# Wider VectorE reductions and ScalarE exponentials in the attention stage of a post-LN layer, and a shorter mask chain

## The reference

```python
q = (x @ wq.T) ... 32 heads of 128;  k, v = 8 heads of 128, each shared by 4 query heads; RoPE on q and k
scores = einsum('bhqd,bhkd->bhqk', q, k) / sqrt(128)
masked = where(causal, scores, NEG)
chunk_max = masked.reshape(b, 32, s, s // 16, 16).max(axis=-1)     # maxima over 16 keys
topk_idx = top_k(chunk_max, 8)                                     # 8 best chunks per query
allowed = causal & (in one of the 8 chunks | k_pos < 128 | k_pos > q_pos - 128)
attn = softmax(where(allowed, scores, NEG))
x = layernorm(x + (attn @ v) @ wo.T)
G = softmax gates of the 16 best of 64 adapters per token (x @ Wr.T)
x = layernorm(x + 2 * sum over adapters of (x @ A.T * G) @ B)
```

## Time and profile before

| what | us |
|---|---|
| median of 2 timed runs (6370.9 and 6371.92) | 6371.41 |
| the profiled execution, its own time | 6302.62 |
| its span, slowest core (core 0) | 6301.0 |
| span of the other cores | 6252.9 to 6294.9 |
| mean granted TensorE clock of core 0 | 0.683 |

### The profile page before, as it was taken

One profiled execution on the slowest core, in us unless ns is written; L12 is line 12 of the kernel. 1 busy time (PEld: TensorE's weight loads), 2 busy tenths in 40 slices (PEclk: granted clock), 3 DMA queues, 4 the chain that ended last, 5 costly groups with the idle time before them and its releaser, 6 DMA issues.

```text
span 6301.0 us, 53967 instructions; the slowest of 8 cores (6252.9 to 6301.0 us)
## 1 busy us (share of the span) xinstructions
PE 3229.1 (51%) x13216; PEld 1286.9 (20%) x13216; DVE 1578.1 (25%) x3829; ACT 1143.7 (18%) x2828; POOL 834.8 (13%) x1700
## 2 busy tenths in 40 slices
PE   5657665656533344445555555555677711275300
PEld 1222222222101111111111222222223311122100
DVE  1120002121343333333333333332000033211223
ACT  0000000000022233333333343443000022100011
POOL 2323332323200000000000000000122200111000
PEclk8889998889755555555555555555888955587755
DMA  7879896868500000000000000001777733464332
GB/s 125 125 108 135 131 141 103 129 104 131 84 6 2 7 1 7 1 7 1 7 1 1 7 1 7 1 1 35 160 170 165 167 122 138 122 142 76 70 133 113
DMA packets 401766, 470.92 MB, mean 75 GB/s; under 512 B 167296, under 2 KB 284032, under 8 KB 395072
## 3 DMA queue, kind: packets, MB, share of 16 engines
q0 software_dynamic: 207360, 252.27, 27.6%
q1 hardware_dynamic: 194112, 215.19, 10.9%
HBM read 652.41 MB, written 67.11 MB: 114 GB/s over the span
## 4 chain that ended last, share of the span: by engine, by line
PE 29%; DMA 23%; DVE 20%; ACT 13%; issue 12%; POOL 1%; DVEq 1%; SPq 1%; ACTq 0%; POOLq 0%; PEldq 0%
ACT Ebuf L475 6%; DMA wqt<-wqT 5%; PE pw L543 5%; PE pq L238 4%; PE pso L340 4%; PE pk L160 3%; PE psS L454 3%; DMA wkvt<-wkT 3%; DMA wkvt<-wvT 3%; DVE Cm L416 3%; ACT Ebuf L484 3%; DMA wot<-woT 3%; PE pB L818 2%; PE psS L464 2%; DVE Cm L419 2%
## 5 line engine op out<-in xcount | busy, mean ns | idle before, releaser
L160 PE MATMUL pk<-xbt,wkvt 128*128 128x512 bf16 x2048 | 504.8, 395 | 198.9 <-DMA wkvt<-wkT 86.2
L238 PE MATMUL pq<-xot,wqt 128*128 128x512 bf16 x2048 | 504.0, 394 | 180.7 <-DMA wqt<-wqT 149.0
L543 PE MATMUL pw<-oft,wot 128*128 128x512 bf16 x2048 | 471.9, 388 | 184.2 <-DMA oft<-oscr 151.6
L320 PE MATMUL ptr<-dgrz,Ebuf 128*128 128x128 bf16 x2304 | 310.2, 303 | 397.8 <-POOL dgrz L403 310.0
L377 PE MATMUL psS<-Kfm,Qfm 128*128 128x512 bf16 (+1 forms) x640 | 327.3, 534 | 285.1 <-ACT Ebuf L475 181.8
L328 ACT CAST PT<-ptr 128x512 bf16<-128x512 f32 (+1 forms) x640 | 322.6, 545 | 619.5 <-PE ptr L320 615.6
L403 POOL TENSOR_SCALAR_AFFINE_SELECT dgrz<-rzb 128x128 bf16<-128x128 bf16 x248 | 72.4, 292 | 2536.8 <-DVE rzb L400 2529.9
L475 ACT ACTIVATE Ebuf<-psS,ngm 128x512 bf16<-128x512 f32 (+2 forms) x512 | 300.5, 587 | 433.2 <-PE psS L464 398.7
L395 DVE TENSOR_REDUCE zz<-zparts 128x1 f32<-128x4 f32 (+4 forms) x248 | 38.7, 156 | 1269.0 <-ACT Ebuf L484 1269.0
L484 ACT ACTIVATE Ebuf<-psS,ngm 128x128 bf16<-128x128 f32 (+2 forms) x352 | 170.0, 483 | 957.9 <-PE psS L377 924.5
L320 PEld LDWEIGHTS ptr<-dgrz,Ebuf 128*128 128x128 bf16 x2304 | 210.1, 131 | 518.4 <-issue 509.2
(11 more groups left out here) (122 smaller groups left out, 3254.4 us busy)
## 6 DMA issues: line engine op xcount, KB each, us to landing
xot<-xoT POOLq DMA_DIRECT2D x256, 256.0 KB, 5.4
oft<-oscr SPq DMA_DIRECT2D x256, 256.0 KB, 4.6
xbt<-xbT POOLq DMA_DIRECT2D x256, 128.0 KB, 5.5
wkvt<-wkT POOLq DMA_DIRECT2D x128, 256.0 KB, 7.3
wkvt<-wvT POOLq DMA_DIRECT2D x128, 256.0 KB, 6.8
wqt<-wqT POOLq DMA_DIRECT2D x256, 128.0 KB, 6.5
wot<-woT POOLq DMA_DIRECT2D x256, 128.0 KB, 4.5
x1t<-x1Tscr SPq DMA_DIRECT2D x96, 256.0 KB, 4.0
```

What stands on the lines that cost most here:

```text
L160: ins = te.matmul(pk[kb][:], wkvt[b][:, kb * 128:(kb + 1) * 128], xbt[b][:], start=(ch == 0), stop=(ch == 31))
L238: ins = te.matmul(pq[ob * 2 + hf][:], wqt[b][:, ob * 128:(ob + 1) * 128], xot[b][:, hf * 512:(hf + 1) * 512], start=(ch == 0), stop=(ch == ...
L320: ins = te.matmul(ptr[j][:, t * 128:(t + 1) * 128], Ebuf[:, kt * 128:(kt + 1) * 128], dgrz[hp][:], start=True, stop=True)
L543: ins = te.matmul(pw[blk * 2 + hf][:], wot[b][:, blk * 128:(blk + 1) * 128], oft[b][:, hf * 512:(hf + 1) * 512], start=(ch == 0), stop=(ch ...
```

## The change

Four edits in the attention loop. The two reductions into `Cm` become one over all Nk columns. The 0/1 mask, its memset and the conversion become one compare-and-multiply that writes `mnegb` directly, followed by a memset of its first 8 chunks to 0. The exponentials of the mid part become one instruction over nmid columns, across banks. Those of the last part become one over W columns. Each bank's `bank_free` is now the last exponential that reads the bank.

```diff
-                    if nmid > 0:
-                        p.w(vec, "ST", ts)
-                        p.w(vec, "SV")
-                        src = psS[:, base: base + nmid].rearrange("p (c k) -> p c k", k=16)
-                        p.inc(vec.tensor_reduce(Cm[:, 0:ncmid], src, AX.X, ALU.max), "SV")
                     p.w(vec, "ST", ts)
                     p.w(vec, "SV")
-                    p.inc(vec.tensor_reduce(Cm[:, ncmid:nch],
-                                            psS[:, base + nmid: base + Nk].rearrange("p (c k) -> p c k", k=16),
+                    p.inc(vec.tensor_reduce(Cm[:, 0:nch],
+                                            psS[:, base: base + Nk].rearrange("p (c k) -> p c k", k=16),
                                             AX.X, ALU.max), "SV")
...
-                    p.w(vec, "SV")
-                    p.inc(vec.tensor_scalar(M01[:, 0:nch], Cm[:, 0:nch], thr[:, 0:1], None, ALU.is_ge), "SV")
-                    p.w(vec, "SV")
-                    p.inc(vec.memset(M01[:, 0:8], 1.0), "SV")
                     p.w(vec, "ST", tmt_prev)
                     p.w(vec, "SV")
-                    p.inc(vec.tensor_scalar(mnegb[:, 0:nch], M01[:, 0:nch], 1.0, 1e30,
-                                            ALU.subtract, ALU.mult), "SV")
+                    p.inc(vec.tensor_scalar(mnegb[:, 0:nch], Cm[:, 0:nch], thr[:, 0:1], -1e30,
+                                            ALU.is_lt, ALU.mult), "SV")
+                    p.w(vec, "SV")
+                    p.inc(vec.memset(mnegb[:, 0:8], 0.0), "SV")
...
-                    for (bank, off, n) in mid_banks:
+                    if nmid > 0:
                         p.w(sc, "SS")
-                        ssv = p.inc(sc.activation(Ebuf[:, off:off + n], psS[:, base + off: base + off + n],
+                        ssv = p.inc(sc.activation(Ebuf[:, 0:nmid], psS[:, base: base + nmid],
                                                   AF.Exp, bias=ngm[:, 0:1],
                                                   accum_out=zparts[:, zcol:zcol + 1]), "SS")
                         zcol += 1
-                        bank_free[(base + off) // 512] = ("SS", ssv)
-                    off = nmid
-                    while off < Nk:
-                        n = min(512 - (base + off) % 512, Nk - off)
-                        p.w(sc, "SS")
-                        ssv = p.inc(sc.activation(Ebuf[:, off:off + n], psS[:, base + off: base + off + n],
-                                                  AF.Exp, bias=ngm[:, 0:1],
-                                                  accum_out=zparts[:, zcol:zcol + 1]), "SS")
-                        zcol += 1
-                        bank_free[(base + off) // 512] = ("SS", ssv)
-                        off += n
+                        for bank in range(base // 512, (base + nmid + 511) // 512):
+                            bank_free[bank] = ("SS", ssv)
+                    p.w(sc, "SS")
+                    ssv = p.inc(sc.activation(Ebuf[:, nmid:Nk], psS[:, base + nmid: base + Nk],
+                                              AF.Exp, bias=ngm[:, 0:1],
+                                              accum_out=zparts[:, zcol:zcol + 1]), "SS")
+                    zcol += 1
+                    for bank in range((base + nmid) // 512, (base + Nk + 511) // 512):
+                        bank_free[bank] = ("SS", ssv)
```

## The result

| | before | after |
|---|---|---|
| median of the timed runs, us | 6322.07 (10 runs, 6299.84 to 6371.92) | 6064.88 (11 runs, 6049.82 to 6136.97) |
| profiled execution, us | 6302.62 | 6064.88 |
| span of the slowest core, us | 6301.0 | 6063.3 |
| mean granted clock, slowest core | 0.683 | 0.689 |
| instructions, VectorE / ScalarE | 3829 / 2828 | 3349 / 2060 |

The ratio is 0.9599, with a 95% interval of 0.9557 to 0.964: the change takes 4.0% off. Against the profiled execution the forecast was 6070 us, 5 more than the 6064.88 measured.

What follows compares the result with a forecast made beforehand. Attention was taken as a serial per-head loop bound by waits. Part A 126 plus part B 107 gave 233 us: 6302.6 to 6070 us profiled, or 6371.4 to 6138 us timed, range 6080 to 6195.

Steps and rivals of the forecast that it cites:

- What bounds the kernel: Attention stage: waiting, not throughput; one serial loop per head through PE, DVE and ACT, 13.2 us in unit 7.
- Part A: Fewer exponentials in attention: 27 to 15 per head over the units, 0.44 us for each removed, 126 us in all.
- the give-back in units 4 to 7: Banks come free together, so score matmuls stand in a row at 0.427 us; unit 7 gains 0.81 instead of 1.32.
- The estimate by the Trainium skill: Back-to-back exponentials overlap by some 93 ns; a removed one is worth about 0.19 us, the sum some 95 us less.
- the score matmuls take 0.38 instead of 0.58 in those heads: 6 us more: In 8 of 32 heads, after attention-times-V at clock 0.99, the matmul row costs half: 6 us more gain.
- the first rival: Clock rises sooner, half-way through attention-times-V's 16 matmuls: 50 us more saved, 6088 us; chance 0.07.
- Part B: Maxima and mask on VectorE: 0.26 us plus 0.33 us off heads without attention-times-V, 107 us in all.
- The level: Two timed runs' median, 6371.4 us, 69 above the profiled execution; saving taken over unchanged, giving 6138 us.
- the common release: Rival: banks released together eat part A's saving in units 4 to 7; 135 us saved, 6236 us; chance 0.06.
- part B was not hidden: Rival: PT copies or transposes hide part B, leaving part A alone, 6245 us; chance 0.04.
- the half rate: Rival: ScalarE reads across banks at half the rate, +184 us, 6322 us, no change to tell; chance 0.03.
- the slower case: Multi-bank exponentials run at a third of the rate, +369 us, 6507 us; chance 0.02.

Runs made afterwards that it cites:

- e1: Only the merged exponentials of the change, on the kernel before, with maxima and mask as before; ratio 0.9789 to the kernel before.
- e5: Changed kernel with the two exponentials of a head in units 1 to 3 made one over all Nk columns; ratio 0.9516 to the kernel before.
- e6: Changed kernel with the two exponentials of units 4 to 7 cut at column 1024 instead of nmid; ratio 0.9588 to the kernel before.
- e10: Changed kernel plus idle matmuls in units 5 to 7, only before the next scores where attention-times-V comes next; ratio 0.9538 to the kernel before.
- e3: Only the two reductions made one, on the kernel before; ratio 0.9927 to the kernel before.
- e4: Only the compare-and-multiply and the memset of mnegb, on the kernel before; ratio 0.9926 to the kernel before.
- e12: The kernel before run once more, unchanged; median 6360.11 us beside 6368.1, ratio 0.9994, profiled execution 6357.43 us.
- e2: Only the VectorE edits (one reduction, shorter mask chain), on the kernel before, exponentials as before; ratio 0.9817 to the kernel before.
- e11: e5 plus idle matmuls in units 4 to 7 behind the cneg matmul, before the mask and before the next scores; ratio 0.9291 to the kernel before.
- e8: Changed kernel plus idle matmuls (6 per plain head before the mask, 3 to 8 before the next scores); ratio 0.9641 to the kernel before.

## Why the prediction was right or wrong

- **What bounds the kernel**: right. The loop through PE, DVE and ACT has the form described, in the waits and in the timeline after.
- **Part A's prices**: right. 0.44 us for a removed exponential, 0.834 ns a column across banks (1647 ns for 1664), and the give-back in units 4 to 7 (e1, e5, e6). The estimate by the Trainium skill ("ScalarE: Activation LUTs", What ACT_TABLE_LOAD costs), about 0.19 us each, did not hold in this loop; in e5 each of 96 removed exponentials took 0.44 or 0.45 us off its head.
- **Part A's sum**: too small, 126 against 143 measured. The failed term is "the score matmuls take 0.38 instead of 0.58 in those heads: 6 us more". It took the moment of the clock's rise as given. The AV heads of units 5 to 7 lost 1.4 to 2.1 us each in e1. This is the first rival, which was held to be another case with 50 us: it came in part, beside the forecast. With the whole change it shows in units 6 and 7 (AV heads 1.51 and 2.68 us shorter) and not in units 4 and 5 (0.34 and 0.33, less than part A alone promised), so part of the good sum is luck. That work in front of attention-times-V brings the rise forward was shown by e10; that it was the row of score matmuls which did so in e1 is suggested by e6 and not proved.
- **Part B**: right in place and price (0.26 and 0.33 us, e3 and e4), 6 us too large in sum (107 against 101), with AV heads that grew by up to 0.9 us.
- **The sum for the profiled execution**: 233 us, against 238 measured there and 247 in the attention stage alone. The agreement to 5 us is partly luck: the other stages happened to take 9 us more.
- **The level**: this is the step that failed and put the time outside the range: "The two timed runs have a median of 6371.4, 69 us above it; I take the saving over unchanged". These were the highest two of ten runs whose median is 6322.07. Of the 73 us between forecast and result 49 are this level; the other 24 are the saving, 257 us between the two medians instead of 233, and the interval of the ratio (228 to 280 us) holds both. In the profiled pair 14 of them are seen in the attention stage (247 instead of 233). 6322.07 less 233 is 6089, inside the range; the measured ratio times 6371.4 is 6116, inside too. As a ratio the forecast was 0.963, inside the measured interval. The profiled execution at 6302.6 stood 69 us lower and said that the level was uncertain by as much as that. The range had a term for each price and none for this. In the one pair of executions that e12 gives, the difference lies in the stages around attention, not in the loop that changed; why they took longer stays open.
- **The other rivals**: the common release costs what the row of matmuls costs and no more (e6); part B was not hidden in plain heads (174 of 224 waits, 0.55 to 0.60 us each in e2); wide reads run at the normal rate on ScalarE, so neither the half rate nor the slower case came.

## What to carry to other kernels

In a loop that passes through several engines, an instruction removed is worth its fixed part with the accumulator read behind it, here 0.44 us on ScalarE and 0.26 on VectorE, if the loop waits for it and for nothing behind it; merging pieces that release buffers one by one gives part of this back, so cut at the buffer's edges where a consumer could start. Write the forecast as a ratio, and let the spread of the base runs into the range. Where TensorE runs at 1.2 GHz in a chain of waits, its clock is a larger term than the instructions: idle matmuls in its gaps gave 137 us here (e11 against e5), where there were enough of them to hold the clock, and cost time where there were not (unit 1 of e8, 267 us instead of 216).

## What the runs showed of the hardware

- One ACTIVATE reads four PSUM banks at the rate of one: 1647 ns for 1664 columns, 687 for 512. One `tensor_reduce` over 2048 columns in four banks takes 2292 ns, against 1892 and 558 for its two parts.
- A compare with a pointer operand and a second operation by a constant costs what the compare costs alone: 287 ns for 128 columns, against 286 for L430's form.
- The moment at which the clock rises moves with changes that leave TensorE's own instructions alone. Sixteen matmuls of 512 columns took between 3.61 and 6.57 us in this study. In unit 7 they took 5.95 us or more in every head of e6 and 3.61 in three of eight with the change, and a gain of 13 us was cancelled so.
- An ACTIVATE that leaves a row sum is followed by a read of the accumulator of 0.19 us, and the next one starts 0.87 us after it for a duration of 0.69.
